# Routed experts in units of 256 and 128 rows, sixteen of them placed by six batches' counts, with five batches of the shared network behind them

## The reference, cut to what matters

```python
# 8 batches of 512 tokens, 128 channels
x = x + ga * attention(layernorm(x) * (1 + ca) + sa)          # 16 heads
h = layernorm(x) * (1 + cb) + sb
shared = (silu(h @ Wg) * (h @ Wu)) @ Wd                        # 128 -> 256 -> 128, all tokens
top2 = the two of 8 experts with the largest sigmoid(h @ router + bias); weights normalised to 1
routed = sum over the two experts e of  w_e * (silu(h @ G_e) * (h @ U_e)) @ D_e
x = x + gb * (shared + routed)
```

## Time and profile before

| what | value |
|---|---|
| timed runs, us | 681.18, 681.9, 684.36 (median 681.9) |
| profiled execution: span, us | 683.7 |
| instructions | 11593 |
| busy share of the span | PE 91%, DVE 76%, ACT 60%, POOL 39% |
| mean granted TensorE clock | 0.971 |
| last attention product ends | 483.4 us |
| first `unit_up` starts | 532.55 us |
| last result evacuated by ACT | 657.9 us |
| last indirect send issued | 661.9 us |

### The profile page before, as it was taken

The page is one execution under the profiler, slowest core; times in us unless marked ns, Lnnn a source line. Parts: engine busy times, 40 slices in busy tenths (PEclk is TensorE's granted clock), DMA queues, the critical chain, the costliest instruction groups (busy, mean ns, idle before and its releaser), DMA issues.

```text
span 683.7 us, 11593 instructions
## 1 busy us (share of the span) xinstructions
PE 624.5 (91%) x3693; PEld 298.9 (44%) x3693; DVE 516.7 (76%) x1104; ACT 411.0 (60%) x846; POOL 264.0 (39%) x309
## 2 busy tenths in 40 slices
PE   4988999999999999999999999999998898888935
PEld 2332333233333333433333333232465888888931
DVE  5659888889988989888898888983368655555617
ACT  2145777777777687777777777778542445444520
POOL 4221022324352461452434233134434366566540
PEclk9669999999999999999999999999999999999987
DMA  3533132222321233223222231115102222222228
GB/s 101 146 56 97 52 101 76 66 82 72 94 86 62 75 97 95 79 78 105 72 70 75 70 98 52 39 40 173 53 0 70 64 74 78 69 78 79 70 68 320
DMA packets 50064, 56.92 MB, mean 83 GB/s; under 512 B 10281, under 2 KB 39243, under 8 KB 50004
## 3 DMA queue, kind: packets, MB, share of 16 engines
q1 hardware_dynamic: 42648, 43.11, 22.4%
q0 software_dynamic: 4320, 8.47, 3.6%
q10 hardware_dynamic: 3036, 4.61, 2.1%
HBM read 38.36 MB, written 17.92 MB: 82 GB/s over the span
## 4 chain that ended last, share of the span: by engine, by line
PE 68%; DVE 13%; ACT 6%; DMA 4%; issue 4%; SPq 2%; POOL 1%; another core or an unknown queue 0%; ACTq 0%; POOLq 0%; DVEq 0%
PE pv L1457 15%; PE st L1446 14%; PE mx L1431 13%; PE st L1646 9%; DVE neg_max L1012 6%; PE mx L1590 3%; ACT pt L803 2%; PE misc L1324 2%; PE misc L1351 2%; PE pv L1655 2%; PE misc L1655 2%; PE st L1600 1%; PE misc L1357 1%; DMA even_qk<-k_parts 1%; DVE ln L969 1%
## 5 line engine op out<-in xcount | busy, mean ns | idle before, releaser
L803 ACT ACTIVATE pt<-st 128x512 f32<-128x512 f32 x496 | 282.2, 598 | 106.0 <-PE st L1446 96.8
L1012 DVE TENSOR_REDUCE neg_max<-mx 128x2 f32<-128x1024 f32 x248 | 294.4, 1215 | 50.5 <-PE mx L1431 47.3
L1457 PE MATMUL pv<-pt,vs 128*32 128x512 f32 x1024 | 136.4, 605 | 0.3 <-ACT pt L803 0.3
L690 POOL DMA_INDIRECT routed<-rec,row_u x64 | 64.4, 1007 | 142.1 <-PE pv L1457 115.2
L750 POOL DMA_INDIRECT results<-qs,home_u x71 | 77.4, 1091 | 60.5 <-ACT qs L932 42.1
L1446 PE MATMUL st<-even_qk 74*128 74x512 bf16 x256 | 88.9, 388 | 4.1 <-DMA even_qk<-m_rows 2.2
L1446 PE MATMUL st<-qs,ks 74*128 74x512 bf16 x240 | 81.5, 383 | 1.8 <-ACT pt L803 1.1
L1431 PE MATMUL mx<-even_qk 72*128 72x512 bf16 x240 | 74.5, 392 | 6.0 <-DVE neg_max L1012 3.4
L1431 PE MATMUL mx<-ks,qs 72*128 72x512 bf16 x256 | 76.5, 380 | 2.8 <-DVE neg_max L1012 2.5
L1258 DVE TENSOR_TENSOR vs<-vs,st 128x256 f32<-128x256 f32 x71 | 29.7, 418 | 42.6 <-ACT vs L927 31.4
L1646 PE MATMUL st<-vs,pt 128*128 128x128 f32 x376 | 52.0, 282 | 10.3 <-DVE vs L1258 7.4
(11 more groups left out here) (199 smaller groups left out, 792.7 us busy)
## 6 DMA issues: line engine op xcount, KB each, us to landing
ks<-routed SPq DMA_DIRECT2D x71, 65.0 KB
even_qk<-q_parts SPq DMA_DIRECT2D x48, 96.0 KB
qs<-q_parts SPq DMA_DIRECT2D x48, 96.0 KB
ks<-k_parts SPq DMA_DIRECT2D x48, 96.0 KB
even_qk<-k_parts SPq DMA_DIRECT2D x42, 96.0 KB
q_parts<-qk_parts SPq DMA_DIRECT2D x21, 128.0 KB
k_parts<-qk_parts SPq DMA_DIRECT2D x7, 384.0 KB, 2.3
x_in<-L_attn_x SPq DMA_DIRECT2D x8, 256.0 KB
```

What stands on the lines that cost most here:

```text
L690: pool.indirect_dma_start(out=routed_dram, out_offset=bass.IndirectOffsetOnAxis(ap=row_u[:, k, t:t + 1], axis=0), in_=rec[b.par][:, k, t, ...
L803: act.activation(pt[n % 2][:, hh, :], score_bank(b, n, hh), ACT.Exp, scale=SCALE).then_inc(exp_done, 1)
L1012: dve.tensor_reduce(neg_max[g % 2][:, hh, 2 * half:2 * half + 2], mx_bank[half][:], AX_X, ALU.max, negate=True).then_inc(mx_free, 1)
L1457: last = pe.matmul(pv_bank[32 * hh:32 * (hh + 1), :], vs[b.par][:, j, HG * g + hh, :], pt[n % 2][:, hh, :], start=(n % Y_SLOTS == 0), stop ...
```

## The change

Units come in two sizes. The first 28 are pairs, 256 rows of one expert; the last 15 have 128 rows. The sizes are fixed when the program is built; which expert a unit serves and where it begins is worked out on the chip. The capacity is the same: 28 x 2 + 15 = 71 blocks of 128 rows. All tiles of a unit are twice as wide for a pair: one transposition bank with 256 columns, `up` in the two halves of a two-bank tile, two down projections, two scaled evacuations, and two indirect sends. A unit's load is one DMA. The act ring is 3 instead of 4.

The first 16 pairs hold rows of batches 0 to 5 only. Their tables (`early_tables`) are worked out on DVE in slots 8, 9, 10 and 12 of the last attention batch. Their loads on SP wait for those tables, for the scatters of batches 0 to 5 and for the last score matmul. The rest of the rows, of all batches, fill the 12 other pairs and the 15 single units; their tables (`late_tables`, five parts) stand in DVE's order after the multiplications of units 7 to 11, and the 8 padding DMAs stand in SP's order ahead of the loads of units 13 and 14. The router, choice and row numbers of the last batch move into the steps of the first units, and its scatter stands in POOL's order ahead of the send of unit 4.

The shared network runs for batches 0 to 2 ahead of the units, and for batches 3 to 7 after them, over three pairs of banks. For those, DVE adds the two results, adds the down projection, multiplies by gb and adds to x1 (`finish`); for batches 0 to 2 it adds the two results, multiplies and adds (`finish_first`). PE no longer adds results. SP alone loads the results and stores the outputs.

```diff
-UNITS = K_TOP * TOKENS // P + E
-MOST_UNITS = K_TOP * TOKENS // P + E - 1
-ARING = 4
+ARING = 3
+PAIR = 2 * P
+EARLY_PAIRS, LATE_PAIRS = 16, 12
+PAIRS = EARLY_PAIRS + LATE_PAIRS
+UNITS = PAIRS + K_TOP * TOKENS // P + E - 1 - 2 * PAIRS
+FIRST_SHARED = 3
...
+        def halves(u):
+            return 2 if u < PAIRS else 1
...
-        OUT_ORDER = (0, 2, 1, 4, 3, 6, 5, 7)
+        OUT_ORDER = (3, 0, 4, 1, 5, 2, 6, 7)
...
+            sp.wait_ge(early_ready, 1)
+            sp.wait_ge(rows_free, 2 + B - 2)
+            sp.wait_ge(st_full, HG * SLOTS * B)
+            for u in range(UNITS):
+                if u == 13:
+                    pad_regions(range(0, E // 2))
+                if u == 14:
+                    pad_regions(range(E // 2, E))
+                if u == EARLY_PAIRS:
+                    sp.wait_ge(padding_written, 16 * (E + 1))
+                    sp.wait_ge(scattered, BATCH_ROWS * B)
+                    sp.wait_ge(tables_ready, 2)
+                if u == PAIRS:
+                    sp.wait_ge(tables_ready, 3)
+                load_unit(u)
+            for slot in range(RING):
+                sp.wait_ge(yu_sent[slot], 16 * sends(slot, UNITS))
+            for b in OUT_ORDER:
+                for k in range(K_TOP):
+                    sp.dma_start(results[b][k], result_v[:, k, b]).then_inc(results_loaded[b], 16)
+            for place, b in enumerate(OUT_ORDER):
+                sp.wait_ge(out_ready, place + 1)
+                sp.dma_start(out_v[:, b], x1[:, TT * b:TT * (b + 1), :]).then_inc(out_stored, 16)
...
 # POOL, behind the loop
             scatter(B_LAST.plus(-1))
             rstd(mv2, ve2, var2_ready, rstd2, rstd2_ready, stats2_ready, B_LAST)
+            rows_scattered(B_LAST.plus(-1))
             modulate2(B_LAST)
-            scatter(B_LAST)
+            def send_unit(u):
+                slot = u % RING
                 hold(pool, yu_ready, u + 1)
+                for h in range(halves(u)):
+                    pool.indirect_dma_start(out=result_dram, out_offset=bass.IndirectOffsetOnAxis(ap=home_u[:, slot, h:h + 1], axis=0),
+                                            in_=y_u[slot][:, h, :], in_offset=None, bounds_check=K_TOP * TOKENS - 1,
+                                            oob_is_err=False).then_inc(yu_sent[slot], 16)
+            for u in range(UNITS):
+                if u == 4:
+                    scatter(B_LAST)
+                send_unit(u)
...
 # DVE, behind the loop
+            dve.wait_ge(routed_loaded, 64)
+            dve.wait_ge(early_ready, 2)
+            experts = experts_of(0)
+            for u in range(2):
+                unit_weights(u, experts)
             shared_act(2, 1)
             shared_sum(1)
+            layer_norm2(B_LAST)
+            for u in range(2):
+                unit_rows(u)
             shared_sum(2)
+            for i in range(UNITS):
+                ahead = i + 2
+                if ahead < UNITS:
+                    if ahead == EARLY_PAIRS:
+                        dve.wait_ge(tables_ready, 4)
+                    if ahead % RING == 0:
+                        experts = experts_of(ahead // RING)
+                    unit_weights(ahead, experts)
+                unit_act(i)
+                if ahead < UNITS:
+                    unit_rows(ahead)
+                if i == 2:
+                    add_router_bias(B_LAST, use(B_LAST, "lg_last"))
+                if i == 3:
+                    likeliest(B_LAST)
+                if i == 4:
+                    choose(B_LAST)
+                if i == 6:
+                    assign_rows(B_LAST, use(B_LAST, "rank_last"))
+                if i in (7, 8, 9, 10, 11):
+                    late_tables(i - 7)
...
+            def finish(b):
+                r = results[b][0]
+                add_results(b)
+                dve.wait_ge(s_down, b + 1)
+                dve.tensor_tensor(r, down_bank(b)[:].rearrange("p (t c) -> p t c", t=TT), r, ALU.add).then_inc(s_gated, 1)
+                dve.wait_ge(s_gated, b + 1)
+                gate_and_add(b)
...
 # PE, behind the loop
             shared_up(2, 0)
             shared_up(2, 1)
             shared_dn(1)
+            unit_T(0)
             shared_dn(2)
+            unit_T(1)
+            pe.wait_ge(routed_loaded, 64)
+            for i in range(UNITS + 2):
+                if i < UNITS:
+                    unit_up(i)
+                if i + 2 < UNITS:
+                    unit_T(i + 2)
+                if i == UNITS + 1:
+                    pe.wait_ge(misc_free, use(B_LAST, "rank_last") + 1)
+                    shared_up(FIRST_SHARED, 0)
+                if i >= 2:
+                    unit_dn(i - 2)
+                if i == 1:
+                    h2_T(B_LAST, use(B_LAST, "h2T_last"))
+                if i == 2:
+                    router_logits(use(B_LAST, "lg_last"))
+                if i == 6:
+                    ranks(B_LAST, use(B_LAST, "rank_last"))
+            shared_up(FIRST_SHARED, 1)
+            for j in range(IC):
+                shared_up(FIRST_SHARED + 1, j)
+            shared_dn(FIRST_SHARED)
+            for b in range(FIRST_SHARED + 2, B):
                 for j in range(IC):
                     shared_up(b, j)
                 shared_dn(b - 1)
             shared_dn(B - 1)
```

More of the change, by code:

```diff
@@ L352, in score_bank, with sends, xT_bank, up_bank @@
             return st_bank[hh % 2][:]
-        def sum_bank(b):
-            return mx_bank[b // 2 % 2][:, 1, :]
+        def halves(u):
+            return 2 if u < PAIRS else 1
+        def sends(slot, before):
+            return sum(halves(u) for u in range(slot, before, RING))
+        def xT_bank(u):
+            return pv_bank[:, 0:halves(u) * P]
+        def up_bank(u, which):
+            return mx_bank[u % 2][:, which, 0:halves(u) * I]
+        def y_bank(u):
+            return st_bank[u % 2][:, 0:halves(u) * C].rearrange("p (h c) -> p h c", h=halves(u))
+        def shared_bank(b, j, which):
+            if b < FIRST_SHARED:
+                return mx_bank[j][:, which, :]
+            turn = (IC * (b - FIRST_SHARED) + j) % 3
+            if turn == 0:
+                return (pv_bank, misc)[which][:]
+            return mx_bank[2 - turn][:, which, :]
+        def down_bank(b):
+            return st_bank[(b + 1) % 2]
         def fill_of(f):
@@ L711, in scatter @@
                     scatter_rows(b, i)
-                rows_scattered(b)
             pool.wait_ge(setup_pool, 4)
@@ new lines, in starts, with take @@
+            def starts():
+                step(dve.tensor_tensor(entered[:, 0:E, :], earlier[:], padded[:].unsqueeze(1).to_broadcast([P, E, E]), ALU.mult))
+                step(dve.tensor_reduce(region_end[:], entered[:, 0:E, :], AX_X, ALU.add))
+            def take(rows, into):
+                step(dve.tensor_scalar(into[:], region_end[:], -1.0, float(rows), ALU.mult, ALU.add))
+                step(dve.tensor_scalar(into[:], into[:], 0.0, None, ALU.max))
+                step(dve.tensor_tensor(into[:], into[:], padded[:], ALU.min))
@@ new lines, in early_tables @@
+            def early_tables(part):
+                if part == 0:
+                    dve.wait_ge(misc_free, use(B_LAST.plus(-1), "rank") + 1)
+                    step(dve.tensor_tensor(padded[:], next_row[B % 2][:], first_row[:], ALU.subtract))
+                    whole_blocks(padded[:], padded[:], PAIR, 0.0)
+                if part == 1:
+                    starts()
+                    take(EARLY_PAIRS * PAIR, taken[0])
+                if part == 2:
+                    skips(None)
+                    places(0, EARLY_PAIRS, 2)
+                if part == 3:
+                    rows_from(0, EARLY_PAIRS, 0.0, early_ready)
+                    unit_experts(0, EARLY_PAIRS, early_ready)
@@ L1319, in _ @@
+            for j in range(IC):
+                shared_act(4, j)
+            finish(3)
+            for j in range(IC):
+                shared_act(5, j)
+            finish_first(0)
+            finish(4)
+            for j in range(IC):
+                shared_act(6, j)
+            finish_first(1)
+            finish(5)
+            for j in range(IC):
+                shared_act(7, j)
+            finish_first(2)
+            finish(6)
+            finish(7)
         @block.tensor
@@ L1630, in _ @@
                 shared_dn(b - 1)
-            def unit_T(u, slot, turn):
-                pe.wait_ge(xu_loaded[slot], 16 * (turn + 1))
-                pe.transpose(mx_bank[0][:, slot % 2, 0:P], xu[slot][:, 0:C], ident[:]).then_inc(xuT_full, 1)
-            def unit_up(u, slot, wait):
-                pe.wait_ge(xuT_ready, u + 1)
-                if wait:
-                    pe.wait_ge(act_ready, u - 1)
-                else:
-                    pe.wait_ge(w_ready, u + 1)
-                for m in range(2 * IC):
-                    last = pe.matmul(st_bank[slot % 2][:, m * P:(m + 1) * P], w_unit[u % WRING][:, m * P:(m + 1) * P], xuT[slot % 2],
```

(2 more changed lines are left out.)

448 lines of the change are left out of this document (202 added, 246 removed).

## The result

The changed kernel takes 675.0 us (median of 4 runs, 672.7 to 676.8) against 682.6 (4 runs, 681.2 to 684.4) for the kernel before in the same session: ratio 0.988, 95% interval 0.984 to 0.992. The forecast was 650, range 638 to 668. The direction was right; about a quarter of the forecast gain came. In the chain of waits PE has 67% of the span, DVE 12% and "another core or an unknown queue", 0% in the earlier trace rows, 2%.

What follows compares the result with a forecast made beforehand. PE was taken to bound the kernel up to the end, where DVE does. Last send at 620, plus 5.3, 24.0 and 2.4 us, gave 651.7 in the span, 650 on the median, range 638 to 668.

Steps and rivals of the forecast that it cites:

- Start of the units: After shared batches 0 to 2, PE's first up starts at 502.2 us, against 532.55 before the change.
- A pair's pace: Unit stage on PE: a 256-row pair costs 2.83 us at full pace, against 2.90 for two units.
- PE's pauses: Unit stage: pauses on top of PE's floor of 604.6 us, bringing PE's end to 616.7.
- DVE's wait for the send of unit 4: Step 10 of the units: DVE waits for that send, landing near 538 where its turn is near 537.
- POOL: Unit stage: scatter until 534, then 63 sends of 1.35 us, 85 us, to 619; 620 taken for the last send.
- that reading: POOL's sends: half as many DVE copies bring sends to 1.28 us, 81 us for 63, POOL done at 615.
- The end: After the last send: 5.3 us to DVE's first add, 24.0 of DVE work, 2.4 of last store.
- The sum: Whole kernel: 651.7 us span against 683.7, 32.0 less; 650 on the median.
- ACT's late starts: Unit stage: typically 2.34 us before a silu, cause unread; against 2.5 us slack in pairs, 1.0 in singles.
- the second: Rival, unit stage: pauses belong to time, tables and padding cost in full; 664 us span, 662 median; chance 0.28.
- Its worst end: Unit stage, pauses-by-time rival: PE ends at 616.7 + 15 + 12.6 = 644 us.
- The third: Rival, POOL's sends bound and get dear: 1.78 us each gives 678, from 1.87 no gain; chance 0.05.

Runs made afterwards that it cites:

- a1: The changed kernel unchanged, on one more chip, a quiet one: 650.5 us against 664.5 for the kernel before, ratio 0.977.
- e6: The change's order with all 71 units of 128 rows, no pairs: 670.1 us, ratio 1.009 to the kernel before, on a quiet chip.
- f6: Changed kernel with 16 slots of row numbers, ACT waiting for sends eight back, pads before loads 14 and 15; quiet chip: 655.8 us, ratio 0.985 to the kernel before.
- after: The changed kernel's first session and profile, on a disturbed chip: 675.0 us against 682.6 for the kernel before, ratio 0.988.
- a2: The changed kernel unchanged, on a further chip, a disturbed one: 676.7 us against 685.4 for the kernel before, ratio 0.989.
- f4: Changed kernel without each pair's second send, result rows prefilled with x during attention; disturbed chip: 657.0 us against 687.6 for the kernel before, ratio 0.955.
- e2: Changed kernel with padding rows written by ScalarE's queue in the first two attention batches instead of SyncE's eight padding DMAs; quiet chip: 677.5 us.

## Why the prediction was right or wrong

Its steps, against a1 (quiet) and the first profile (disturbed):

- Start of the units, 502.2: 501.65 and 502.58. Right on both.
- A pair's pace, 2.83 us: 2.84 on both where nothing is late. Right.
- PE's pauses, 12 us in all (singles 4.6, pairs 2, tables 2.5, table loads 0.5, pads 2.5): on a1 PE stands 4.5 us in the unit stage. The pauses of over half a us are 1.17, at a load behind the pads, and 2.62, which the wait for a send and a part of the tables make together; none is at single units. The last unit's down is over at 613.65, forecast 616.7. Too many where the chip is quiet. On the disturbed chip PE stands 24.3 us, 15.0 of them before 600, nearly all in pairs.
- DVE's wait for the send of unit 4 near 538: 539.10 on a1, 3.94 us. Named, and priced at nothing; with the part of the tables behind it, it costs PE 2.6.
- POOL: scatter from 523.7 (a1: 524.0), then 63 sends. I took 1.35 each; they follow at 1.31 (82.7 us to 616.8), and one takes 1006 ns as the mean of all on a1, against 1091 in the earlier trace rows. This is what the Trainium skill (SBUF — State Buffer, "SBUF: two separate sides") lets one expect with fewer float32 copies on DVE (43 for 71), and a1's last send at 616.8 lies nearer the 615 of that reading than 620. The traces bear it out: in the kernel before the 50 sends that overlap such a copy take 1.14 us on average and the 21 others 0.98, and all 31 sends of over 1.03 us are among the 50; e6, with 71 copies again, has 1053 ns, f6, with 43, 1027. No run takes the copies alone away.
- The end, 5.3 + 24.0 + 2.4: 4.6 + 23.7 + 2.5 on a1, 4.6 + 24.0 + 2.4 on the first chip. Right.
- The sum: 651.7 in the span, 650 in the median. a1 has 647.5 and 650.5. The span is 4.2 us under the forecast: 3.2 by a last send that ends sooner, 1.0 by the end. The near hit of the median is part luck: the forecast took the median 1.8 us below the span, from the span of the profiled execution and the median of the timed runs, but each run's time stands some 1.8 us above its own span (649.3 for 647.5 in a1's profiled run).

So on a quiet chip the terms come out within some us, the pauses as too large, and the time with them. What failed on the measured chip is the step from ACT's late starts to PE: "A pause of 2.3 us therefore reaches PE today and mostly doesn't in a pair", which put the pauses of the pairs at 2 us. It took 2.3 us as the length of a late start and set 2.5 us of slack against it. The length isn't fixed. It grows with the run of indirect DMAs on POOL, and the change gives POOL a run of 14 and after it a duty of 2.57 in 2.84 us. The counts for y then come 15.0 us late behind the run of 14 and 3.1 to 4.5 behind the runs of six, which the slack doesn't cover: PE stands 24.3 us in the unit stage in place of 12. The sum also had no term for the clock: PE works 114.3 us there, where it works 107.5 on a1, some 7 us more, in the stretches at the lower clock behind its pauses. And on POOL's side it had the 63 sends without a rest, 85 us; they take 107.3, as POOL waits for y.

Of the 32 us that I subtracted, some 18 were the disturbance in the kernel before (682.6 to 664.5), which I counted as gone; 14 are the change's own (664.5 to 650.5). On the disturbed chip the first 18 don't come and the changed kernel pays 6 to 7 more.

The rivals: the second (pauses belong to time, 662) had the right sign and the wrong law; by time PE would have lost 22 of every 125 us, but it lost none in 502 to 531, 12 in the next 29, and with half the sends 0.8 in 40. Its worst end, PE done at 644 and so some 678 in the span, is near the 641.2 and 675.0 that came, by a law that isn't the right one. The third asked for dear sends: they became cheaper, 1.09 to 1.00 us, yet on the disturbed chip the sends do set the pace, one in 1.67 us, through the waits between them. Its breakeven of 1.87 us was not far.

What stays open: what makes a chip or a session disturbed (the path on which PE's counts and SP's instructions meet POOL's descriptors wasn't seen), whether SP's loads and pads take part, the pads in the hole above all, and how the 0.70 us steps arise.

## What to carry to other kernels

A pause whose cause the trace doesn't show can't be carried into a sum as a fixed length: ask what else is running in each of its instances (here POOL's queue, in all of them), and give the sum twice, with it and without. A trace comes from one chip; two sessions can differ by 3.6% for the same kernel (663.8 and 687.6) while ratios within a session hold, and a change may be worth 1.2% on one chip and 2.3% on another. Where an in-order queue takes a block of extra work, compare how long it holds up the next transfer with the time from where that one would have landed to the moment its place is asked for, and not with the length of the whole ring: 10.1 us against 6.2 cost PE 2.6, 13.8 against 2.9 cost it 11.4.

## What the runs showed of the hardware

- In some sessions (after, a2, f4) a matmul's semaphore count moves up to 15 us late while GpSimd issues indirect DMAs back to back, and several held counts then move together within 0.32 us, in TensorE's order; in the hole SyncE's register instructions slow to 0.70 us each. In a quiet session 75 such DMAs in a row make no count over 0.2 us late (e2). ACT's signals to DVE stay prompt in both (silu over at 534.30, DVE starts at 534.33 in the hole).
- Most late counts move 0.9 to 2.4 us after the last DMA of the run; a few move while it goes on (533.70, 536.56 and 614.98 in the first profile). Counts are 1.9 us late at a run of three (kernel before), 3.1 to 4.5 at runs of six, 10.7 at one of ten (f4) and 15.0 at one of fourteen.
- An indirect DMA of 128 rows holds GpSimd for 0.97 us plus 0.30, whether it goes on for one or for 75, and 1.14 us on average where a 768-column copy of DVE overlaps it (kernel before); a memset of 352 columns behind each adds 0.26 (its own 0.43 hides a part of the 0.30).
